# A decoder block with routed experts on one core: the routing of rows cut into other pieces and placed elsewhere

## The reference, cut to what matters

```python
x = layernorm(x + attn(x, Wk, Wv, Wo, freqs))      # x: 16 x 128 x 256, a rotated running sum
x = layernorm(x + xattn(x, ctx, ctx))              # scores with a decay, 128 x 128 for each batch row
x = layernorm(x + ffn(x, router_w, up, down))

def ffn(x, router_w, up_proj, down_proj):          # 2048 rows of 256, 8 experts, the best 2 of each row
    probs = softmax(x @ router_w.T)
    scores, expert_idx = top_k(probs, 2)
    gate = scores / sum(scores)
    h = x @ up_proj[e]                             # for each chosen expert e: 256 -> 512
    hidden = silu(h[:256]) * h[256:]
    out = sum of gate * (hidden @ down_proj[e])    # 256 -> 256
```

## Time and profile before

| | |
|---|---|
| median of 3 runs | 253.44 us (252.93 to 253.65) |
| the profiled execution | 254.41 us, span from first to last instruction 252.6 us |
| PE busy | 198.1 us (78% of the span) |
| DVE busy | 170.1 us (67%) |
| ACT busy | 129.8 us (51%) |
| POOL busy | 112.5 us (45%) |
| chain that ended last | PE 53%, DVE 26%, DMA 7%, issue 6% |

### The profile page before, as it was taken

One profiled execution on the slowest core, in us unless ns is written; L12 is line 12 of the kernel. 1 busy time (PEld: TensorE's weight loads), 2 busy tenths in 40 slices (PEclk: granted clock), 3 DMA queues, 4 the chain that ended last, 5 costly groups with the idle time before them and its releaser, 6 DMA issues.

```text
span 252.6 us, 4975 instructions
## 1 busy us (share of the span) xinstructions
PE 198.1 (78%) x1264; PEld 172.4 (68%) x1264; DVE 170.1 (67%) x575; ACT 129.8 (51%) x356; POOL 112.5 (45%) x108
## 2 busy tenths in 40 slices
PE   8698699999889898867897888999999999800000
PEld 7577589979677797746786677888888888700000
DVE  4855977897869885858977844565656565405992
ACT  2333445644445333435564655767676767520474
POOL 1076154545537666003775674343434343436900
PEclk9889999999999999979999999999999999985555
DMA  7965357456274213032435665323232322029634
GB/s 223 381 231 200 106 186 238 139 207 210 92 242 156 77 64 107 22 87 84 114 119 165 194 198 147 123 87 121 67 113 69 115 80 83 32 52 390 266 125 166
DMA packets 20299, 37.11 MB, mean 147 GB/s; under 512 B 3246, under 2 KB 11697, under 8 KB 20273
## 3 DMA queue, kind: packets, MB, share of 16 engines
q1 hardware_dynamic: 16864, 28.36, 34.8%
q0 software_dynamic: 3408, 8.45, 9.1%
HBM read 25.06 MB, written 12.65 MB: 149 GB/s over the span
## 4 chain that ended last, share of the span: by engine, by line
PE 53%; DVE 26%; DMA 7%; issue 6%; ACT 3%; SPq 2%; POOL 1%; ACTq 0%; DVEq 0%; POOLq 0%
PE p_c L542 12%; PE p_v L542 6%; PE p_s L542 4%; PE p_c L448 4%; PE p_a L542 4%; PE p_v L432 4%; DMA keep<-rows_dram 3%; PE p_y L568 3%; DVE keep L899 3%; PE p_t L581 3%; PE p_s L475 2%; DVE st L902 2%; PE p_a L516 2%; PE p_y L493 2%; PE p_v L405 2%
## 5 line engine op out<-in xcount | busy, mean ns | idle before, releaser
L1038 POOL DMA_INDIRECT rows_dram<-x_rows,dest_idx x32 | 31.8, 994 | 29.5 <-DVEq L721 20.8
L854 DVE TENSOR_TENSOR parts<-p_y,parts 128x256 fp32r<-128x256 f32 x39 | 16.6, 425 | 28.1 <-ACT parts L979 27.3
L542 PE MATMUL p_c<-w_hi,parts 128*128 x104 | 34.6, 414 | 0.0
L1054 POOL TENSOR_TENSOR w_lo<-keep,w_hi 128x1536 fp32r<-128x1536 f32 x6 | 20.6, 3442 | 12.0 <-ACT x_rows L947 12.0
L568 PE MATMUL p_y<-const,keep 128*128 128x128 f32 x78 | 15.6, 282 | 10.3 <-DVE parts L854 5.1
L1048 POOL TENSOR_TENSOR space<-back 128x512 f32<-128x512 f32 x8 | 10.1, 1268 | 26.2 <-DVE back L808 26.2
L1071 POOL DMA_INDIRECT y_dram<-x1T,put_idx x14 | 13.6, 975 | 17.8 <-ACT x1T L996 13.9
L1071 POOL DMA_INDIRECT y_dram<-angle,put_idx x12 | 11.7, 974 | 17.6 <-ACT angle L996 13.4
L542 PEld LDWEIGHTS p_c<-w_hi,parts 128*128 128x128 f32 x104 | 17.7, 189 | 2.5
L1071 POOL DMA_INDIRECT y_dram<-x2T,put_idx x13 | 12.7, 975 | 14.1 <-ACT x2T L996 12.5
L448 PE MATMUL p_c<-const,space 128*128 128x128 f32 x128 | 16.6, 284 | 2.4 <-DVE space L662 2.4
(11 more groups left out here) (154 smaller groups left out, 525.8 us busy)
## 6 DMA issues: line engine op xcount, KB each, us to landing
keep<-in_weights SPq DMA_DIRECT2D x8, 768.0 KB, 6.4
keep<-rows_dram SPq DMA_DIRECT2D x39, 129.5 KB, 2.1
w_hi<-y_dram SPq DMA_DIRECT2D x8, 512.0 KB, 7.4
space<-in_xT SPq DMA_DIRECT2D x8, 256.0 KB, 3.0
keep<-in_x SPq DMA_DIRECT2D x8, 256.0 KB, 3.9
space<-in_ctxT SPq DMA_DIRECT2D x8, 256.0 KB, 4.1
space<-in_ctxt SPq DMA_DIRECT2D x8, 256.0 KB, 2.7
out<-x_rows SPq DMA_DIRECT2D x8, 256.0 KB, 2.4
```

Of the source, the lines that this page charges most:

```text
L542: last = nc.tensor.matmul(dst, lhs[:, k, :], w[:].rearrange("p e n -> p (e n)")[:, bass.ds(start + col + k * width, width)], start=(n == 0 ...
L854: nc.vector.tensor_tensor(xs_lo[(k + 1) % RING], p_xt, xs_hi[(k + 1) % RING].bitcast(F32), ALU.subtract).then_inc(xlo_ok, 1)
L1038: nc.gpsimd.indirect_dma_start(rows_dram, bass.IndirectOffsetOnAxis(ap=dest_idx[:, c, b:b + 1], axis=0), x2_rows[:, b, :], None, bounds_ch ...
L1054: nc.gpsimd.tensor_tensor(w_lo[:, i, :], w_in[s], w_hi[:, i, :].bitcast(F32), ALU.subtract).then_inc(lo_ok, 1)
```

## The change

Four things are moved; no instruction is added or dropped.

1. `list_tiles(0)`, the list of the first phase, stands right behind `count_tiles(0)`, one pipeline step earlier.
2. `choose(2, 0)`, `choose(2, 1)` and `mark(2)` leave the place ahead of the first tile and stand inside DVE's `tile(0)`, between the helpers of tile 1 and hid(0). PE's `place(2)` goes from the end of `tile(0)` into `tile(1)`, behind up(1).
3. The later routing pieces on DVE are cut smaller and spread: `destinations(2)` from tile 0 to 1; the count and list of phase 1 from tiles 1 and 2 to tiles 2 to 5; `choose(3, ...)` from 3 and 4 to 6 and 7; `destinations(3)` from tile 6 to 8; the count and list of phase 2 from tiles 7 and 8 to tiles 9 to 12. PE's `place(3)` goes from the end of tile 5 into tile 8.
4. POOL issues the sends of group 2 as four ahead of put(0) and four ahead of put(1) (before: two behind each of four later places), and those of group 3 in pairs at tiles 9 to 12 (before 7 to 10).

```diff
@@ PE, tile(k), behind the up product
+                if k == 1:
+                    pe.wait_ge(logits_ok, PAIRS)
+                    place(2)
+                if k == 8:
+                    pe.wait_ge(place_read, 3)
+                    place(3)
@@ at its end
-                if k == 0:
-                    pe.wait_ge(logits_ok, PAIRS)
-                    place(2)
-                if k == 5:
-                    pe.wait_ge(place_read, 3)
-                    place(3)
@@ DVE, at_step
                 if where == (8, 2):
                     dve.wait_ge(zeros_ok, 7)
                     count_tiles(0)
+                    list_tiles(0)
                 if where == (9, 2):
-                    list_tiles(0)
                     low_part(7)
-                    choose(2, 0)
@@ DVE, ahead of tile(-1)
-            choose(2, 1)
-            mark(2)
@@ DVE, tile(k), ahead of hid(k)
+                if k == 0:
+                    choose(2, 0)
+                    choose(2, 1)
+                    mark(2)
@@ DVE, tile(k), behind hid_lo(k-1)
-                if k == 0:
+                if k == 1:
                     destinations(2)
-                if k == 1:
+                if k == 2:
                     pass_over(0)
-                    count_tiles(1)
-                if k == 2:
-                    list_tiles(1)
+                    count_done(1)
                 if k == 3:
+                    count_upto(1)
+                if k == 4:
+                    list_experts(1)
+                if k == 5:
+                    list_rows(1)
+                if k == 6:
                     choose(3, 0)
-                if k == 4:
+                if k == 7:
                     choose(3, 1)
                     mark(3)
-                if k == 6:
+                if k == 8:
                     destinations(3)
-                if k == 7:
+                if k == 9:
                     pass_over(1)
-                    count_tiles(2)
-                if k == 8:
-                    list_tiles(2)
+                    count_done(2)
+                if k == 10:
+                    count_upto(2)
+                if k == 11:
+                    list_experts(2)
+                if k == 12:
+                    list_rows(2)
@@ POOL, tile(k), ahead of put(k-2)
+                if k in (2, 3):
+                    send(4 * k + 8, 4 * k + 12)
+                if k in (9, 10, 11, 12):
+                    send(2 * k + 6, 2 * k + 8)
@@ POOL, behind put(k-2)
-                if k in (1, 2, 3, 4):
-                    send(2 * k + 14, 2 * k + 16)
-                if k in (7, 8, 9, 10):
-                    send(2 * k + 10, 2 * k + 12)
```

More of the change, by code:

```diff
@@ L725, in count_tiles, with count_done @@
             def count_tiles(g):
-                starts = first_tile[g]
+                count_done(g)
+                count_upto(g)
+            def count_done(g):
                 bias = HALF if g == 2 else -HALF
@@ L730, in count_tiles, with count_upto @@
                 link(nc.vector.tensor_scalar(done[:], part[:], ROUND, -ROUND, ALU.add, ALU.add))
+            def count_upto(g):
+                starts = first_tile[g]
                 link(nc.vector.tensor_tensor(upto[0][:, E:], done[:], starts[:, 0:E], ALU.subtract))
@@ L737, in list_tiles, with list_experts @@
             def list_tiles(g):
+                list_experts(g)
+                list_rows(g)
+            def list_experts(g):
                 n = PHASES[g]
-                starts = first_tile[g]
                 row = const[:, C_ROW:C_ROW + n]
@@ L747, in list_tiles, with list_rows @@
                 link(nc.vector.tensor_reduce(expert[:, 0:n], past[:, 0:n, :], AX_X, ALU.add))
+            def list_rows(g):
+                n = PHASES[g]
+                starts = first_tile[g]
+                row = const[:, C_ROW:C_ROW + n]
                 link(nc.vector.scalar_tensor_tensor(tile_at[:, 0:n], leaps[:, 0:n], starts[:, 0:1], row, ALU.add, ALU.add))
```

## The result

The changed kernel is slower. Its median is 259.71 us over 4 runs (257.86 to 260.41), beside 253.40 us of the kernel before, 6.3 us more. The same kernel again, with the experiments on another occasion, gave 1.0106 (1.0034 to 1.0177). One of its four executions, the profiled one, took 261.46 us, 1.9% above the fastest, and is outside that ratio. The profiled execution of the first set took 257.86 us and was the fastest of its four; it is 3.45 us above the profiled one of before (254.41), and its span is 256.1 us, 3.5 more. I forecast 4.0 more.

What follows compares the result with a forecast made beforehand. PE bounds stage 2 from 154, so xt(14) decides: first fill 139.7 + clock 1.0 + SP's run 12.9 + load 2.9 = 156.5, 4.0 us later. Median 253.44 + 4.0 = 257.4 us, range 255.3 to 259.2.

Steps and rivals of the forecast that it cites:

- when xt(14) starts: Last late transpose in stage 2, behind which PE does not wait: 156.5 against 152.47, 4.0 us later.
- Start: Start of stage 2: xs_lo(0) 1.2 us earlier, hid(0) at 114.2, eighth send at 128.2, tile 9 at 133.9 against 135.9.
- fill_idx: Written only after tile 9 lands, 138.7 against 133.3, so SP's first fill leaves at 139.7, 3.5 us later.
- The clock: PE's clock falls in the wait for tile 9, costing 1.0 us (bounds 0 and 1.3); rival "stays up": 256.4, chance 0.30.
- SP's run: From first fill to load 14 on SP's queue: 12.9 us, bounds 12.3 and 13.4; then load 14 takes 2.9 us.
- The last sends: Rival: group 3's late sends bring load 17 at 165.5 instead of 163, 1.5 us on top, 259; chance 0.08.

Runs made afterwards that it cites:

- start-only run: Kernel before with only the first list behind its count, the choice of group 2 in tile 0 and place(2) in tile 1: ratio 1.0041, median 255.43 us.
- sends-only run: Kernel before with only the eight sends of group 2 issued as four ahead of put(0) and four ahead of put(1): ratio 0.9952.

## Why the prediction was right, by its own steps

**The question was when xt(14) starts.** Right for the profiled execution: 3.4 us later for a time 3.45 us longer, and no wait behind it. That execution was the fastest of its set, so a match of 3.45 with the 4.0 forecast says less than it seems; the medians of that set are 6.3 us apart. In the profiled execution of the second set xt(14) was not the last wait, xt(17) was.

**Start.** xs_lo(0) 1.4 us earlier (forecast 1.2), hid(0) at 114.06 (114.2), last destination at 117.09 (117.1), eighth send at 128.16 (128.2), xt(9) at 133.98 (about 134). The start-only run shows no net gain from the earlier xs_lo(0) with its later destinations; the sends-only run shows the eight sends worth 0.5% by themselves. Together they give tile 9 the 2.0 us forecast. With group 3 back at its old tiles that is a gain of 0.7 to 1.4% (0.9925 and 0.9862).

**fill_idx.** Shown: with group 3 at its old tiles the kernel turns from slower to faster, and with only SP's wait moved two tiles on, most of the loss goes while `fill_idx` stays late. The first fill was at 140.21, forecast at 139.7 and, with the clock, 140.7. Of the 0.5 us between, 0.3 lie ahead of the end of the writing, where place(3) stood between up(8) and the transposes for 0.2 us and not the 0.4 estimated, and 0.2 behind it: SP's transfer left 0.8 us after the writing, not 1.0.

**The clock.** It fell, at a cost of 0.7 us in up(8), where I had 1.1, as it fell only in the middle of it, and of 1.0 us on the whole way to `fill_idx`, the number that I took. That it adds as much to the time is not shown: filling the wait did not shorten it measurably.

**SP's run.** 13.3 us, where I took 12.9 and should have kept 13.4. The 3.37 us that I gave as load to load was the shortest of three steps in the trace before (3.37, 3.81 and 3.99), and no run shows the 12.3 that I had as lower bound: over the runs with this order it was 13.2 to 14.7. The landing of load 14 was 2.3 us instead of the 2.9 that I kept. That these two errors, 0.4 up and 0.6 down, nearly cancel is luck; with the 0.5 of the first fill they make 155.87 for a forecast of 156.5.

**The last sends.** I had them hidden by about 1 us and gave them 8 in 100. In the profiled execution they were: the last send left at 157.08, for 157, load 17 at 160.74, and PE came to it 2.9 us later. But a margin of 1 us is less than the spread of a landing, 2.0 to 4.0 us, and I gave the landing no spread. In the second set's profile it cost 1.04 us, with the fills later 1.73 us; with group 3 late on the kernel before, where the load left only 0.2 us ahead of PE, 2.08 us plus a fallen clock.

**Small slips in the working.** The 106.28 from which I took the 15 chained instructions stands in no row: the chain has 106.32 and the timeline 106.24, which leaves 3.2 to 3.3 us. The lower end of the range is 253.44 + 1.8 = 255.2, not 255.3. Its second 0.6 us, a shorter landing of load 14, is not the 0.8 of the text above it; the landing measured is shorter by 0.6. For a gain of 0.8 us `fill_idx` would have to be written by 134.4, not 134.6. None of them changes the forecast.

**What stays open.** The median of the first set lies 1.85 us above its own profiled execution, beyond the upper end of my range by 0.5 us, and 2.3 us above my number; the ratio of the second set gives 2.7 us of loss, less than forecast. The profiles show where an execution can lose a microsecond: the start of stage 2 (1.6 us), landings of a tile between 2.0 and 4.0 us, SP's run between 13.2 and 14.7 us, and a wait at tile 17. The one of 261.46 us has some of each. But none was taken of the first set's executions of 259.5 to 260.4, taking the last sends forward did not lower the median beside the second set, and the cause of the first set's extra time is not shown.

## What to carry to other kernels

A piece of work that is spread out on an engine with little slack moves behind whatever that engine waits for next: before moving it, look for the last semaphore that it raises and for a queue that stops at it. Here one small cast, put behind the arrival of a tile, held a queue in which the loads of later tiles stood, though the cast served only other transfers. Where a queue holds both urgent transfers and ones that can wait, the second kind can stand later, but not so late that their own reader waits: with the fills two tiles later most of the loss went, and with the last fill ahead of tile 17 PE waited 1.41 us for that tile. What comes next in the queue's order, here the sends for tile 17, is the next bound and should be costed as well, with the spread of a landing and not its usual value.

## What the runs showed of the hardware that I had not expected

- A float32 matmul of 128 x 128 on 128 columns took 5.36 / 24 = 0.22 us with the clock at 2.4 GHz, in the run with 24 unread matmuls, and stands as two records in the profile (24 of them as x48); I had read the records as matmuls.
- The landing of the same transfer, a tile of 129.5 KB from DRAM, took 2.05 us in one place and 3.95 us in another (the load of tile 9 in the start-only run, that of tile 17 with the fills later), a spread of 1.9 us, as much as most terms of the sum.
